# Edges of the second type counted during the max pass, beside its gathers, in place of the third pass

## The reference

```python
x = ln(x + L0(x))     # GIN: sum of h[src] over the edges, two dense layers
x = ln(x + L1(x))     # two normalised sum convolutions, 128 -> 256 -> 128
x = ln(x + L2(x))     # msgs = z[dst]@Wd + z[src]@Ws + weight*ww + bm
                      # agg = segment_max(msgs, dst); then two dense layers
x = ln(x + L3(x))     # m_data or m_ctrl by edge type, segment_sum, + self, relu
```

## Time and profile before

| | us |
|---|---|
| median of 3 runs | 3555.3 (3551.98 to 3558.2) |
| the profiled execution | 3554.84 |
| its span | 3550.9 |
| PE busy in the span | 2963.4 (83%) |
| POOL busy | 2358.4 (66%) |
| DVE busy | 1691.7 (48%) |
| ACT busy | 961.2 (27%) |

### The profile page before, as it was taken

One profiled execution on the slowest core, in us unless ns is written; L12 is line 12 of the kernel. 1 busy time (PEld: TensorE's weight loads), 2 busy tenths in 40 slices (PEclk: granted clock), 3 DMA queues, 4 the chain that ended last, 5 costly groups with the idle time before them and its releaser, 6 DMA issues.

```text
span 3550.9 us, 59220 instructions
## 1 busy us (share of the span) xinstructions
PE 2963.4 (83%) x21866; PEld 2101.1 (59%) x21866; DVE 1691.7 (48%) x3971; ACT 961.2 (27%) x2510; POOL 2358.4 (66%) x2323
## 2 busy tenths in 40 slices
PE   3899987899998999999957777878778849888887
PEld 2455554566566888888736566666666635444444
DVE  8566665233333333333346666666666642332332
ACT  2566665232333333333311111111111210000000
POOL 4766553666645666666557777777777746777776
PEclk7899999999998999999978999898888879999999
DMA  6555544767657777777653333333333366566564
GB/s 171 181 179 185 170 158 169 230 203 237 198 173 236 269 264 253 272 254 272 213 160 81 88 89 89 89 89 89 88 89 89 96 206 221 197 203 202 190 205 128
DMA packets 282357, 619.22 MB, mean 174 GB/s; under 512 B 58988, under 2 KB 193429, under 8 KB 274647
## 3 DMA queue, kind: packets, MB, share of 16 engines
q1 hardware_dynamic: 175926, 370.37, 30.5%
q0 software_dynamic: 104416, 243.61, 24.0%
q10 hardware_dynamic: 1728, 1.38, 0.1%
HBM read 472.64 MB, written 142.52 MB: 173 GB/s over the span
## 4 chain that ended last, share of the span: by engine, by line
PE 47%; POOL 21%; issue 9%; DMA 8%; DVE 8%; ACT 6%; SPq 0%; DVEq 0%; ACTq 0%; POOLq 0%
PE banks L1573 27%; POOL arena L442 16%; DMA ring_of_rows<-message_pieces,span_sources 5%; POOL ring_of_rows L1639 5%; PE banks L480 4%; PE banks L1593 4%; PE banks L1591 3%; PE banks L1078 2%; PE banks L392 2%; PE banks L455 1%; ACT junk L529 1%; PE banks L2299 1%; PE banks L1688 1%; DMA arena<-tab_l,ring_of_rows 1%; ACT arena L1906 1%
## 5 line engine op out<-in xcount | busy, mean ns | idle before, releaser
L1573 PE MATMUL banks<-arena 128*128 128x384 bf16 (+1 forms) x9212 | 1500.3, 312 | 27.5 <-DVE arena L1797 15.8
L1573 PEld LDWEIGHTS banks<-arena 128*128 128x128 bf16 x9212 | 883.0, 99 | 458.8 <-issue 53.8
L442 POOL DMA_INDIRECT arena<-tab_l,ring_of_rows x831 | 809.0, 974 | 295.3 <-issue 249.0
L1639 POOL DMA_INDIRECT arena<-h_pieces,span_sources x450 | 448.1, 996 | 274.2 <-PE banks L1593 134.9
L1639 POOL DMA_INDIRECT ring_of_rows<-message_pieces,span_sources x450 | 482.3, 1072 | 192.9 <-issue 109.7
L392 PE MATMUL banks<-arena 128*128 x1758 | 385.6, 322 | 175.7 <-DVE arena L419 91.7
L392 PEld LDWEIGHTS banks<-arena 128*128 128x128 f32 x1758 | 292.3, 217 | 240.3 <-issue 238.7
L1639 POOL DMA_INDIRECT ring_of_rows<-x_pieces,span_sources x270 | 302.6, 1121 | 193.0 <-PE banks L1591 125.3
L419 DVE TENSOR_TENSOR arena<-arena,banks 128x129 f32 x879 | 250.7, 285 | 328.9 <-PE banks L392 250.7
L1591 PE MATMUL banks<-ring_of_rows,arena 128*128 128x384 bf16 x990 | 286.1, 339 | 132.0 <-DMA ring_of_rows<-message_pieces,span_sources 121.5
L1639 POOL DMA_INDIRECT ring_of_rows<-l_pieces,span_sources x270 | 269.2, 997 | 184.6 <-PE banks L1591 95.4
(11 more groups left out here) (245 smaller groups left out, 3135.2 us busy)
## 6 DMA issues: line engine op xcount, KB each, us to landing
arena<-edge_counts SPq DMA_DIRECT2D x82, 896.0 KB, 5.6
arena<-edge_counts SPq DMA_DIRECT2D x82, 672.0 KB
edge_counts<-arena SPq DMA_DIRECT2D x34, 1568.0 KB
typed_counts<-arena SPq DMA_DIRECT2D x24, 1568.0 KB, 6.7
arena<-scan_mask SPq DMA_DIRECT2D x208, 128.0 KB
arena<-typed_counts SPq DMA_DIRECT2D x24, 896.0 KB, 7.5
arena<-typed_counts SPq DMA_DIRECT2D x24, 672.0 KB
arena<-tab_l,ring_of_rows POOLq DMA_INDIRECT x831, 2.6
```

The lines of the kernel that those rows point to most:

```text
L442: k.nc.gpsimd.indirect_dma_start(k.RG3[:, i % RING, at:at + width], None, table, bass.IndirectOffsetOnAxis(ap=k.SRC[:, i:i + 1], axis=0)). ...
L1573: t = T.matmul(k.bank[i % N_SUMS][:, 0:rows.shape[-1]], counts[:, s, :], rows, start=s == 0 and n == 0, stop=s == NT - 1 and n == len(term ...
L1639: G.indirect_dma_start(k.rows[p.layer][s % n], None, k.pieces[p.layer], bass.IndirectOffsetOnAxis(ap=k.SRCG[:, at:at + 1], axis=0)).then_i ...
```

## The change

The typed counts leave `l1b` and are made in the regular program of `l2`. Chunk `c` from 3 on does unit `c - 3`, until 192 are done. On PE the unit stands between `steps(slots[c][2])` and the transposes back; on ACT its casts follow the copy of the chunk; on DVE a quarter's comparisons stand in every second chunk ahead of the last slot; on SP the store and the next keys stand ahead of a mask. The ring of the max pass is 32 slots in place of 64; the rest of its memory holds two typed slabs, keys and one-hots. The units use PSUM banks 5 and 7; the nodes' "parts" of the max pass move to banks 4 and 6. Bases of steps are folded into 32 slots once, in `l0`. Three loads (sources, places, bases) move from the end of `l1b` to its start, and its gathered rows alternate between two banks.

```diff
+REGULAR_RING = 32
+TYPED_FROM = 3
+        self.ring = REGULAR_RING if regular else RING
@@ tensor_l2
         steps(k.slots[c][2])
+        if p.regular and typed_unit(c):
+            tensor_typed_counts(k, *typed_unit(c))
         T.wait_ge(k.sem("l2_scanned"), c + 1)
...
     steps(k.slots[NCH][0])
+    if p.regular:
+        T.wait_ge(k.sem("typed_units"), UNITS * len(TYPED))
@@ vector_l2
         steps(k.slots[c][2])
         message((c + 2) * CH + 3)
+        if p.regular and c + 2 >= TYPED_FROM and (c + 2 - TYPED_FROM) % 2 == 0:
+            vector_typed_one_hots(k, (c + 2 - TYPED_FROM) // 2)
         steps(k.slots[c][3])
@@ scalar_l2
-        if c * CH + CH > AHEAD:
-            A.wait_ge(p.product, c * CH + CH - AHEAD)
+        if c * CH >= p.ring:
+            A.wait_ge(p.product, p.last_step_of(chunk_tiles(c)[-1] - p.ring) + 1)
         A.copy(k.RG3[:, slot:slot + n, 0:H], wide(k.bank[BACK][:, 0:n * P], P)).then_inc(k.sem("l2_back_copied"), 1)
+        if p.regular and typed_unit(c):
+            scalar_typed_counts(k, *typed_unit(c))
         steps(k.slots[c][3])
@@ sync_l2
+    def load_keys(i):
+        if i < len(TYPED):
+            if i >= 2:
+                S.wait_ge(k.sem("typed_onehot"), 4 * (i - 1))
+            at = TYPED[i] * TILE_PAIRS * 2
+            for n in range(2):
+                S.dma_start(k.KEYS[i % 2][:, n * 2 * TILE_PAIRS:(n + 1) * 2 * TILE_PAIRS],
+                            k.keys_dram[n][:, at:at + 2 * TILE_PAIRS]).then_inc(k.sem(f"load_keys_{i % 2}"), 16)
+
+    def store_typed(i):
+        S.wait_ge(k.sem("typed_units"), UNITS * (i + 1))
+        S.dma_start(k.typed_dram[i], k.TSLAB[i % 2].rearrange("p s d -> p (s d)")).then_inc(typed_slab_stored(k, i)[0], 16)
...
     for c in range(NCH):
+        if p.regular and typed_unit(c - 2) and typed_unit(c - 2)[1] == UNITS - 1:
+            store_typed(typed_unit(c - 2)[0])
+            load_keys(typed_unit(c - 2)[0] + 2)
         if c + 2 < NCH:
             load_mask(c + 2)
@@ dense_tensor_l1b
-            i = p.from_matrix.index(j)
-            if q < TYPED_AT:
-                tensor_typed_counts(k, i, 2 * q)
-            tensor_sums(k, p, j, q, lambda i, s: [(slab(k, "l1b", i), k.XP1[:, s, n, :]) for n in range(3)],
-                        (lambda: tensor_typed_counts(k, i, 2 * q + 1)) if q < TYPED_AT else None)
+            tensor_sums(k, p, j, q, lambda i, s: [(slab(k, "l1b", i), k.XP1[:, s, n, :]) for n in range(3)])
@@ dense_vector_l1b, dense_scalar_l1b, dense_sync_l1b
-        if kind == "matrix" and 1 <= q <= TYPED_AT:
-            typed_one_hots(4 * p.from_matrix.index(j) + q + 1)
-            typed_counts(p.from_matrix.index(j), 2 * q)
-            typed_counts(p.from_matrix.index(j), 2 * q + 1)
-            store_typed(p.from_matrix.index(j))
-            load_keys(p.from_matrix.index(j) + 2)
```

More of the change, by code:

```diff
@@ L385, in tensor_step @@
         T.load(k.pe_regs, k.BASES[0:1, s:s + REGS])
-    base = T.snap(k.pe_regs[s % REGS], min_val=0, max_val=(RING - 1) * SLOT)
+    base = T.snap(k.pe_regs[s % REGS], min_val=0, max_val=(p.ring - 1) * SLOT)
     if s % OH_BATCH == 0:
@@ L1026, in store_messages, with message_banks, typed_unit, typed_slab_stored @@
         store(k, p, ("l3", "l3b")[n], g, k.pieces["l3"].rearrange("(t p k) c -> k p t c", p=P, k=2)[n][:, gslice(g), :], pieces, e)
+def message_banks(g):
+    return (banks_of(g)[0], banks_of(g)[2]) if len(banks_of(g)) == 4 else banks_of(g)
+def typed_unit(c):
+    n = c - TYPED_FROM
+    return divmod(n, UNITS) if 0 <= n < UNITS * len(TYPED) else None
+def typed_slab_stored(k, i):
+    return k.sem(f"store_slab_{i % 2}"), 16 * (len(COUNTED[i % 2::2]) + i // 2 + 1)
+def tensor_typed_counts(k, i, u):
+    T, unit, quarter = k.nc.tensor, UNITS * i + u, 4 * i + u // 2
+    if u % 2 == 0:
+        T.wait_ge(k.sem("typed_onehot"), quarter + 1)
+    if unit:
+        T.wait_ge(k.sem("typed_units"), unit)
+    for n in range(4):
+        c = (4 * u + n) % QUARTER
+        for h in range(2):
+            at = slice(REC * h, REC * h + REC)
+            t = T.matmul(k.bank[TYPED_BANKS[h]][:, n * KEYS:(n + 1) * KEYS], k.TSRC[quarter % 2][at, c, :],
+                         k.TKEY[quarter % 2][at, c, :], start=True, stop=True)
+    t.then_inc(k.sem("typed_counted"), 1)
@@ L1029, in tensor_l2, with scalar_typed_counts @@
+def scalar_typed_counts(k, i, u):
+    A = k.nc.scalar
+    A.wait_ge(k.sem("typed_counted"), UNITS * i + u + 1)
+    if u == 0 and i >= 2:
+        A.wait_ge(*typed_slab_stored(k, i - 2))
+    nodes = k.TSLAB[i % 2][:, :, 16 * u:16 * u + 16].rearrange("p s (i h r) -> p s i h r", h=2, r=2)
+    for h in range(2):
+        t = A.copy(nodes[:, :, :, h, :], k.bank[TYPED_BANKS[h]][:, 0:4 * KEYS].rearrange("p (i s r) -> p s i r", i=4, r=2))
+    t.then_inc(k.sem("typed_units"), 1)
 def tensor_l2(k, p):
@@ L1074, in turn_messages @@
         for q, i in enumerate(tiles):
-            rows, turned = k.RG3[:, i % RING, UP:UP + H], k.bank[TURN][:, q * P:(q + 1) * P]
+            rows, turned = k.RG3[:, i % p.ring, UP:UP + H], k.bank[TURN][:, q * P:(q + 1) * P]
             if p.regular:
@@ L1304, in sync_l2 @@
     if p.regular:
+        for i in (len(TYPED) - 2, len(TYPED) - 1):
+            S.wait_ge(*typed_slab_stored(k, i))
         for i, h in ((0, 0), (0, 1), (1, 0)):
@@ L2532, in dense_sync_l1b @@
             reload(p.from_matrix.index(j) - 1, 1)
-        if kind == "matrix" and q == POS - 2:
-            load_keys(p.from_matrix.index(j) + 2)
         for stage, g in p.due.get(n, ()):
```

123 lines of the change are left out of this document (45 added, 78 removed).

## The result

The changed kernel took 3507.06 us (median of 4 runs, 3492.06 to 3516.46), the kernel before on the same chip 3556.75 us (3551.98 to 3558.48, 4 runs). The ratio is 0.986, with a 95% interval from 0.982 to 0.990: 50 us faster. The forecast was 3512 us in a range from 3472 to 3572.

The account below looks back on a forecast made before the run. The prediction took PE to bound the third pass and POOL's gather issue the max pass, with the loop near. Third pass -85, change-over -3 and max pass +45 made -43 us: 3512 us, range 3472 to 3572.

Parts of the forecast that it names:

- What the third pass gives back: Third pass: removing 192 units, 0.38 us each on PE, and PE's waits ahead of them saves 85 us.
- the change-over: Between third and max pass: three loads leave SP's queue, so the first mask comes earlier; 3 us saved.
- rival 3: Third pass becomes bound by its gathers and gives back only 63 us: 3534 us in total; chance 0.13.
- 75 us to spare: Max pass: PE's waits for gathers, 41.3 + 33.4 us of 1048, taken as slack in the PE, DVE and ACT loop.
- The loop's additions: Max pass, onto a loop of 973 us: units 73 + 14, comparisons 30, stores 24, clock -25; sum 1089 us.
- the clock: Max pass: PE waits less for gathers, so a higher granted clock takes 25 us back from the loop.
- the comparisons: Max pass, DVE: quarters' comparisons total 119 us ahead of scans; a quarter of that, 30 us, falls on the loop.
- the stores: Max pass, SP's queue: masks issued behind 24 typed stores come late, 1 us each, 24 us on the loop.
- Nothing covers them: Max pass, PE: units ahead of the transposes back delay copy, steps and turn; 73 us, plus 14 at lower clock.
- POOL's account: Max pass: comparisons with two SBUF inputs slow POOL's gathers, mean 974 to about 993 ns; 20 us added to 1058.
- The waits: Max pass profile expected: POOL's turn wait 20 to 50 us, PE's gather waits under 35, clock 0.88 to 0.92.
- rival 1: Max pass: DVE's comparisons lie whole on the loop, pass 130 us longer, 3597 us in total; chance 0.17.

Follow-up runs that it names:

- the run with nothing: Changed kernel without any typed units, comparisons, casts, keys or stores in the max pass (computation incomplete): 3469.19 us, ratio 0.974 to the kernel before.

## Why the prediction came out right

The forecast of 3512 us is 5 us from the median, and 20 from the execution that was traced. Its steps were not all as good, and that it came so near is in part luck, as the second and third point show.

- **What the third pass gives back: right.** 85 us and 3 for the change-over were forecast; the first gather of the max pass came 89.7 us earlier, and the run without typed work gave 2.6%. PE is still over 95% busy there and POOL waited 56.5 us for it (some 50 forecast), so rival 3 (bound by its gathers) fell: 617 us in place of 624.
- **"75 us to spare": wrong.** I added the row of PEld (41.3) and the row of PE (33.4) of the earlier trace rows. Both are the same waits: a weight load and the product behind it, released by one gather, as the two lines at the free loop show. The two rows also move together in the other traces: 45.2 us in 42 times and 36.9 in 36 with no typed work, 5.0 in 4 and 3.9 in 3 after. The loop had 41 us to spare, and needed 1007 us by itself, not 973.
- **The loop's additions: too large.** 73 + 14 + 30 + 24 - 25 = 116 us were forecast; the free loop grew by 72, in the quickest execution; in the median one, 15 us longer, it may have been up to 87. By parts: the units 42 in place of 87 less the clock; the comparisons 33 for 30, of which 15 coincide with the units; the stores 11 for 24. With the right spare time and my additions the loop would have come to 1123 us, with both right to 1079. Two errors of 34 and 44 us cancelled but for 10: that is the luck.
- **The unit's price.** "Nothing covers them" was the step behind the 73 us. On the first chip a unit cost the loop 0.22 us, not 0.38. It wasn't that the transposes would have waited for their scan anyway: the turn ahead of the unit has waited for that scan already, and in no trace of the first chip does PE wait ahead of the transposes. Against the run with nothing, between first and last scan, PE's busy time grew by 51 us (831.6 to 883.1), at a granted clock of 0.90 in place of 0.88, and its waits in the steps fell, for DVE's additions from 85.8 to 69.5 us and for ACT's copy from 79.1 to 73.7. So part of a unit's price came back as clock and as shorter waits, and "nothing covers them" failed as far as that. That the place matters was right, as the moved unit showed on the slow chip: 65 us there.
- **POOL's account: right.** Mean gather 995 ns for 993 forecast, and 17 us of the comparisons' cost on POOL for 20. In the trace of the result 90 gathers start under one of these comparisons; together they take 19.4 us more than at 0.945 us each, where the comparisons had 28.2 us still to run. The Trainium skill (SBUF — State Buffer, "Summary: rules for kernel authors") has the second instruction fully blocked until the first finishes, which would have made it 25 by the prediction's estimate; this trace has the partial loss of the earlier trace rows.
- **The waits.** POOL's wait for the turn 24.6 us (20 to 50 forecast), PE's for gathers 5.0, or 8.9 with both rows as I had added them (under 35), clock 0.89 (0.88 to 0.92): all as forecast for the case in which loop and POOL are near each other. Scans 36 us longer for 41.
- **The stores.** I took 1 us each; PE's waits for weights behind them make 0.24 to 0.39 us each, the free loop 0.45. The Trainium skill (DMA: Bandwidth & Descriptors, "Queues, rings and completion order"), which I cited against the move, has a DMA engine take its queues in turn, so that gathers share it with a store's rows. I took from it that they land late; the trace after doesn't show their landing, but PE waited 5.0 us for gathers in the whole pass with the stores and 4.5 without, so nothing of it is felt.
- **The bound itself isn't the same everywhere**, which the prediction didn't consider. Where PE stands still for reasons outside the kernel's waits, the loop has nothing to spare and takes the added work whole, as rival 1 described it (POOL's wait over 100 us, time as before), though for another reason than the comparisons: moving PE's unit alone gave 65 of the some 89 us back. There the forecast, taken as a share of the time, would have been wrong.

## What to carry to other kernels

Before work is moved into a stage with idle time, find the loop that nearly bounds it and measure its spare time once, from one engine's row of waits, not from two rows that show the same wait. Then place the added instructions behind the operations that another engine waits for, not ahead of them: where the loop bounded the pass, that was nearly the whole gain (0.998 to 0.982); where POOL bounded it too, the units cost 3 to 5 us in all, so there was little to win, and the move itself wasn't run there. Look at PE's busy time and clock as well as at the waits, since a denser stream of products can give some of its price back. And time a gain of one or two per cent more than once, in another place or at another time, with the kernel before traced beside it.

## What was not expected of the hardware

- The same program took 3557 us in some runs and 4012 and 4060 us in later ones, 13 to 14% more, with equal durations of a gather (median 944 and 945 ns) and a scan (1278 and 1277). In the max pass PE stood 159 us for nothing that the trace shows (3.0 in the first trace of the same kernel), and the granted clock between the scans was 0.80 in place of 0.88. The cause is open, the chip included.
- The place of 192 small units in PE's order, with the same products, went with a granted clock of 0.77 or 0.81 in the pass, and with 59 us of PE's busy time.
- With the loop's products denser, the clock in the max pass rose from 0.87 to 0.89, and work of 141 us by its single prices (73 + 14 + 30 + 24) cost the loop 72, in the traced execution.
